# State-space chunk sums as three products of split factors, formed at the head of the next step

## What is computed

```python
dlast = jnp.exp(cum[:, :, -1:, :] - cum)
states = jnp.einsum('bcjh,bcjhn,bcjhp->bchpn', dtc * dlast, Bc, xc)
cdec = jnp.exp(cum[:, :, -1, :])
def step(s, inp):
    st, dc = inp
    return (dc[:, :, None, None] * s + st, s)
y_inter = jnp.einsum('bcihn,bchpn->bcihp', Cc * jnp.exp(cum)[..., None], prev)
y = (y_intra + y_inter).reshape(b, l, H, P) + Dp[None, None, :, None] * x
```

## Time and profile before

| | us |
|---|---|
| runs | 2136.83, 2136.99, 2141.14 (median 2136.99) |
| the profiled execution, whole | 2136.12 |
| its span, first to last instruction | 2134.4 |
| TensorE busy | 2080.5 (97%) |
| TensorE weight load | 1548.7 (73%) |
| VectorE busy | 1468.0 (69%) |
| ScalarE busy | 1331.0 (62%) |
| GpSimd busy | 866.3 (41%) |

### The profile page before, as it was taken

The page is one execution under the profiler, slowest core; times in us unless marked ns, Lnnn a source line. Parts: engine busy times, 40 slices in busy tenths (PEclk is TensorE's granted clock), DMA queues, the critical chain, the costliest instruction groups (busy, mean ns, idle before and its releaser), DMA issues.

```text
span 2134.4 us, 33703 instructions
## 1 busy us (share of the span) xinstructions
PE 2080.5 (97%) x12040; PEld 1548.7 (73%) x12040; DVE 1468.0 (69%) x1814; ACT 1331.0 (62%) x2368; POOL 866.3 (41%) x759
## 2 busy tenths in 40 slices
PE   6999999998999999999999999999999999999999
PEld 4644444487777777777777777777777777888887
DVE  4466666284668778778878778687787776555555
ACT  2255555543588887878878787887878783333222
POOL 1001111131147576666757657566676672000000
PEclk9999999999999999999999999999999999999999
DMA  3522222142545555555445455455455457545452
GB/s 132 184 76 68 82 74 62 40 153 89 124 130 163 155 165 160 159 155 178 146 151 177 147 168 161 146 166 168 147 166 169 150 189 258 153 148 148 143 183 89
DMA packets 182781, 305.34 MB, mean 143 GB/s; under 512 B 20416, under 2 KB 96704, under 8 KB 182496
## 3 DMA queue, kind: packets, MB, share of 16 engines
q1 hardware_dynamic: 182624, 303.29, 45.7%
HBM read 249.90 MB, written 53.06 MB: 142 GB/s over the span
## 4 chain that ended last, share of the span: by engine, by line
PE 70%; ACT 2%; DVE 1%; POOL 1%; issue 1%; DMA 0%; DVEq 0%; SPq 0%; POOLq 0%; ACTq 0%
PE ssm_pp L156 16%; PE ssm_pp L158 15%; PE ssm_pp L157 15%; PE ssm_py L1412 5%; PE ssm_py L1407 4%; PE ssm_pstate L1391 4%; PE ssm_turn L1368 2%; PE ssm_py L156 1%; PE ssm_py L158 1%; PE ssm_py L157 1%; PE ssm_pp L1351 1%; PE ssm_pstate L156 1%; PE ssm_pstate L158 1%; PE ssm_pstate L157 1%; PE ssm_turn L156 1%; PE ssm_turn L158 1%
## 5 line engine op out<-in xcount | busy, mean ns | idle before, releaser
L156 PE MATMUL ssm_pp<-xhi,ssm_lo 128*128 128x512 f32 x1192 | 479.4, 402 | 4.2 <-DVE ssm_bc L1636 3.5
L158 PE MATMUL ssm_pp<-xhi,ssm_hi 128*128 128x512 f32 x1192 | 466.0, 391 | 0.0
L157 PE MATMUL ssm_pp<-xlo,ssm_hi 128*128 128x512 f32 x1192 | 465.4, 390 | 0.0
L1524 ACT ACTIVATE ssm_sct<-ssm_cumb,ssm_gpar 128x128 f32<-128x128 f32 x1024 | 313.1, 390 | 69.9 <-DMA ssm_cumb<-dt_sums 48.0
L148 POOL TENSOR_TENSOR ssm_lo<-ssm_raw,ssm_hi 128x512 fp32r<-128x512 f32 x150 | 244.0, 1632 | 91.0 <-ACT ssm_hi L137 91.0
L156 PEld LDWEIGHTS ssm_pp<-xhi,ssm_lo 128*128 128x128 f32 x1192 | 224.0, 188 | 67.5 <-issue 18.7
L1636 DVE SCALAR_TENSOR_TENSOR ssm_xc<-ssm_pp,vectors,ssm_xc 128x1022 f32<-128x1022 f32 (+2 forms) x192 | 245.2, 1277 | 34.7 <-ACT ssm_xc L1478 30.0
L158 PEld LDWEIGHTS ssm_pp<-xhi,ssm_hi 128*128 128x128 f32 x1192 | 224.0, 188 | 48.1
L157 PEld LDWEIGHTS ssm_pp<-xlo,ssm_hi 128*128 128x128 f32 x1192 | 224.4, 188 | 42.7
L1671 DVE TENSOR_TENSOR ssm_sct<-ssm_sct,ssm_cbm 128x1024 f32<-128x1024 f32 x128 | 229.1, 1790 | 28.0 <-ACT ssm_sct L1531 28.0
L1813 POOL TENSOR_TENSOR ssm_go<-ssm_t,ssm_gt 128x512 f32<-128x512 f32 x128 | 165.0, 1289 | 171.1 <-DVE ssm_t L1707 171.1
(11 more groups left out here) (281 smaller groups left out, 4141.9 us busy)
## 6 DMA issues: line engine op xcount, KB each, us to landing
ssm_cumb<-dt_sums SPq DMA_DIRECT2D x96, 1024.0 KB, 5.9
ssm_raw<-w SPq DMA_DIRECT2D x150, 256.0 KB, 5.6
gated<-ssm_go SPq DMA_DIRECT2D x128, 256.0 KB, 4.3
ssm_cumb<-dt_sums SPq DMA_DIRECT2D x32, 512.0 KB, 4.0
ssm_gt<-w SPq DMA_DIRECT2D x64, 256.0 KB, 2.7
ssm_xc<-gated SPq DMA_DIRECT2D x32, 512.0 KB, 4.2
ssm_sct<-gated SPq DMA_DIRECT2D x32, 512.0 KB, 4.2
ffn_raw<-w SPq DMA_DIRECT2D x37, 256.0 KB, 2.7
```

The costliest lines, as they stand in the source:

```text
L156: pe.matmul(out, wlo, xhi, start=start, stop=False)
L157: pe.matmul(out, whi, xlo, start=False, stop=False)
L158: return pe.matmul(out, whi, xhi, start=False, stop=stop)
L1524: i = act.activation(sct[:, s % 2, h, :], cumb[:, s % 2, 0, h, :], ACT.Relu, scale=-1.0, bias=gpar[:, unit, 0, s % NTOK, h:h + 1])
```

## The change

- The state sum leaves scan. chunk_sum(g, s-1) forms it at the head of step s on TensorE, ahead of the first entry, as three float32r products of `bt_hi`, `bt_lo`, `xw_hi`, `xw_lo` (none crosses from one group to the next, since step 15 is a chunk 3).
- `xw` has one buffer instead of two. Its high part is a copy on ScalarE in step s behind a weight's high part and ahead of the lag activations; its low part is a subtraction on GpSimd in step s, behind the gate product of step s-1. Both have one buffer, which belonged to the weights of the time-step projection.
- The transposed B is copied as its high part by ScalarE; VectorE subtracts for its low part ahead of the mask, once a group, and `bt_done` moves to that.
- VectorE's state update of step s-1 moves behind scores of step s and the y sum of step s-1.
- Memory: small buffers of the last norm take other places, and the split of the LoRA product on ScalarE moves from step 14 to step 15 of the last group, with its operands where B's parts were.

```diff
@@ -1011,6 +1011,7 @@
         dt_act, dt_dve, dt_turned, dt_copied, cum_out, par_out = map(
             sem, "dt_act dt_dve dt_turned dt_copied cum_out par_out".split())
         pre_done = sem("pre_done")
+        bt_hi_done, xw_hi_done, xw_lo_done = map(sem, "bt_hi_done xw_hi_done xw_lo_done".split())
         rms_in, rms_sum, rms_std, rms_inv, rms_out = map(sem, "rms_in rms_sum rms_std rms_inv rms_out".split())
         cum_in = [sem(f"cum_in{i}") for i in range(2)]
         g_out = [sem(f"g_out{i}") for i in range(2)]
@@ -1022,7 +1023,8 @@
         gt = sb("gt", [P, 2, CU, T])
         bc = sb("bc", [P, 2, T])
         cc = sb("cc", [P, T])
-        btok = sb("btok", [P, NTOK, N])
+        sbr = lambda n, s: ctx.enter_context(nc.sbuf_tensor(f"ssm_{n}", s, F32R))
+        bt_hi, bt_lo = sbr("bt_hi", [P, NTOK, N]), sbr("bt_lo", [P, NTOK, N])
         cbm = sb("cbm", [P, NTOK, CS])
         gpar = sb("gpar", [P, 2, 3, NTOK, HU])
         cdec = sb("cdec", [P, 2, HU, NTOK])
@@ -1030,7 +1032,8 @@
         sct = sb("sct", [P, 2, HU, CS])
         cecl = sb("cecl", [P, 2, HU, CS])
         xp = sb("xp", [P, 2, CU * P])
-        xw = sb("xw", [P, 2, CU * P])
+        xw = sb("xw", [P, CU * P])
+        xw_hi, xw_lo = dt_feed.hi[:, 0, :], dt_feed.lo[:, 0, :]
         state = sb("state", [P, 2, CU * P])
         t2 = sb("t2", [P, 2, CU, CS])
         go = sb("go", [P, 2, CU, CS])
@@ -1039,9 +1042,10 @@
         na = sb("na", [P, 1])
         lc = sb("lora_coef", [P, 1])
         at_lora = LORA % feed.slots
-        h_hi = (feed.hi[:, at_lora, :], dt_feed.hi[:, 0, :])
-        h_lo = (feed.lo[:, at_lora, :], dt_feed.lo[:, 0, :])
-        rms = sb("rms", [P, 2, (G - 1) * T // P])
+        first_tokens = lambda x: x[:, 0:NC, :].rearrange("p c n -> p (c n)")
+        h_hi = (feed.hi[:, at_lora, :], first_tokens(bt_hi))
+        h_lo = (feed.lo[:, at_lora, :], first_tokens(bt_lo))
+        rms = c.causal[:, 0:2 * ((G - 1) * T // P)].rearrange("p (u n) -> p u n", u=2)
         rms_eps = sb("rms_eps", [P, 1])
         z, e_, dt, da = (xc[:, 1, i, :] for i in range(CU))
         cum = gt[:, 1, 3, :].rearrange("p (n t) -> p n t", n=NTOK)
@@ -1198,6 +1202,7 @@
         o.unit0_summed = lambda eng: eng.wait_ge(t2_done, G * NS - NTOK)
         o.unit1_gated = lambda eng: eng.wait_ge(g_done, G * NS)
         o.unit1_summed = lambda eng, early=0: eng.wait_ge(t2_done, G * NS - early)
+        o.eps = rms_eps
         o.scores_read = lambda eng: eng.wait_ge(y_done, G * NS)
         o.weights_split = lambda eng: eng.wait_ge(feed.lo_done, G * GT + NPRE + 1)
         o.base_copied = lambda eng: eng.wait_ge(pre_done, KT)
@@ -1293,6 +1298,7 @@
                         parameters(g + 1, 0)
                     if last and s == 8:
                         sp.wait_ge(var_out, 2 * (G - 1) * B * 16)
+                        sp.wait_ge(cb_done, G)
                         for unit in range(2):
                             sp.dma_start(rms[:, unit, :], over_partitions(c.var_dram[unit, 0:G - 1])
                                          ).then_inc(rms_in, 16)
@@ -1376,21 +1382,26 @@
                                    start=True, stop=True)
                 mm.then_inc(var_sum, 1)
 
-            def scan(g, s):
+            def chunk_sum(g, s):
+
                 t, ch = s % NTOK, s % NC
-                unit = 1 if s < NTOK else 0
-
                 summed = s >= NTOK or before(g, 0, 1) is not None
                 if ch < NC - 1:
-                    pe.wait_ge(xw_done, g * NCA + (carried(s) + 1))
+                    pe.wait_ge(xw_lo_done, g * NCA + (carried(s) + 1))
                     after(pe, state_done, g * NCA + carried(s))
                     if s == 0:
                         pe.wait_ge(bt_done, g + 1)
                     if s % NTOK == NC and summed:
                         after(pe, var_done, var_before(g, s))
-                    pe.matmul(p_state[:], btok[:, t, :], xw[:, s % 2, :], start=True, stop=True
-                              ).then_inc(states_done, 1)
-                elif summed and s % NTOK < NC:
+                    product(pe, p_state[:], bt_hi[:, t, :], bt_lo[:, t, :], xw_hi, xw_lo, True, True
+                            ).then_inc(states_done, 1)
+
+            def scan(g, s):
+                ch = s % NC
+                unit = 1 if s < NTOK else 0
+
+                summed = s >= NTOK or before(g, 0, 1) is not None
+                if ch == NC - 1 and summed and s % NTOK < NC:
                     pe.wait_ge(state_done, g * NCA + carried(s))
                     pe.wait_ge(sqs_done, g * NS + (0 if s < NTOK else NTOK))
                     squares(unit)
@@ -1440,6 +1451,8 @@
 
             def body(g, last):
                 for s in range(NS):
+                    if s > 0:
+                        chunk_sum(g, s - 1)
                     for e in at(s, last)[:1]:
                         entry(g, e, range(1) if last and e >= NE else range(B))
                     for e in at(s - 1, last):
@@ -1506,12 +1519,18 @@
                 act.wait_ge(bt_turned, g + 1)
                 after(act, states_done, g * NCA)
                 e = ENTRIES.index("turn B")
-                act.activation(btok[:].rearrange("p c n -> p (c n)"), slot(e), ACT.Copy).then_inc(bt_done, 1)
+                act.activation(bt_hi[:].rearrange("p c n -> p (c n)"), slot(e), ACT.Copy).then_inc(bt_hi_done, 1)
 
             def copy_c(g):
                 act.wait_ge(x_done, g * NCV + 2)
                 after(act, cecl_done, g * NCA)
                 act.activation(cc[:], bc[:, 1, :], ACT.Copy).then_inc(c_copied, 1)
+
+            def weighed_high(g, s):
+                if s % NC < NC - 1:
+                    act.wait_ge(xw_done, g * NCA + (carried(s) + 1))
+                    after(act, states_done, g * NCA + carried(s))
+                    act.activation(xw_hi, xw[:], ACT.Copy).then_inc(xw_hi_done, 1)
 
             def lags(g, s):
 
@@ -1544,6 +1563,7 @@
 
                 act.wait_ge(dt_dve, 6 + NTOK)
                 act.wait_ge(tile_done, G * GT + LORA + 1)
+                act.wait_ge(states_done, G * NCA)
                 for b in range(B):
                     act.activation(h_hi[b], pp[:, (NE + LORA) % 2, b, :], ACT.Copy, scale=lc[:, 0:1]
                                    ).then_inc(marks.lora_hi, 1)
@@ -1583,9 +1603,7 @@
                     for e in single(s - 1, last):
                         first_tap(g, e)
                     for e in at(s - 2, last):
-                        if last and e == NE + LORA:
-                            lora_high()
-                        elif last and e >= NE:
+                        if last and e >= NE and e != NE + LORA:
                             copy_pre(e - NE)
                     if s % NC == 0 and s % NTOK > 0 and (s > NTOK or before(g, 0, 1)):
                         copy_squares(g * 2 - 1 + s // NTOK, 1 - s // NTOK)
@@ -1597,6 +1615,9 @@
                     tiles = [r for r in (real(g, e, AHEAD) for e in at(s, last) if is_tile(e)) if exists(r, last)]
                     for r in tiles[:1]:
                         high(r)
+                    weighed_high(g, s)
+                    if last and s == NS - 1:
+                        lora_high()
                     if behind(g, s, 1, last):
                         lags(*behind(g, s, 1, last))
                     if before(g, s, 2):
@@ -1672,6 +1693,12 @@
                                   cbm[:, s % NTOK, :].unsqueeze(1).broadcast_to([P, HU, CS]), ALU.mult
                                   ).then_inc(st_done, 1)
 
+            def b_low(g):
+                dve.wait_ge(bt_hi_done, g + 1)
+                e = ENTRIES.index("turn B")
+                dve.tensor_tensor(bt_lo[:].rearrange("p c n -> p (c n)"), slot(e),
+                                  bt_hi[:].rearrange("p c n -> p (c n)").bitcast(F32), ALU.subtract).then_inc(bt_done, 1)
+
             def scaled(g, s):
 
                 n = g * NS + s
@@ -1741,17 +1768,17 @@
                             mv = dve.tensor_copy(par[:, :, i // 2, i % 2 * NC + q, :],
                                                  dt_bank(i)[:, q, :].rearrange("p (u h) -> p u h", h=HU))
                         mv.then_inc(dt_copied, 1)
+            b_low(0)
             mask(0)
             scaled(0, 0)
 
             def body(g, last):
                 for s in range(NS):
-                    if before(g, s, 1):
-                        advance(*before(g, s, 1))
                     grown(g, s)
                     scores(g, s)
                     if before(g, s, 1):
                         finish(*before(g, s, 1))
+                        advance(*before(g, s, 1))
                     if last and s == 10:
                         dve.wait_ge(rms_in, 32)
                         dve.memset(rms_eps[:], RMS_EPS)
@@ -1764,6 +1791,7 @@
                     for e in single(s - 1, last):
                         conv(g, e)
                     if s == NS - 1 and not last:
+                        b_low(g + 1)
```

(12 more changed lines are left out.)

## The result

The changed kernel took 2144.61 us (median of 11 runs, 2140.15 to 2147.02), the kernel before 2136.83 (11 runs beside them): a ratio of 1.0035, 95% interval 1.0027 to 1.0043. It is slower by 7.8 us. The profiled execution has a span of 2142.9 us against 2134.4.

What follows compares the result with a forecast made beforehand. TensorE, busy all 150.50 us of a full group, was taken as the bound. Seven groups' -1.1 and the last group's +0.5 gave -0.6 us on the profiled run's 2136.12, 0.9 below the median 2136.99: forecast 2136.4, range 2125 to 2149.

Steps and rivals of the forecast that it cites:

- TensorE's arithmetic: State sum on TensorE: f32 product 0.86 us out, three products 0.69 in; 0.165 a sum, 1.98 a group, 15.8 in all.
- rival (d): On TensorE each of three products pays 0.10 us extra for change of form, 0.07 a sum left; about 2145 us; chance 0.06.
- The walk through a middle group: Step-by-step waits at TensorE's heads: stalls give back 1.8 of 1.98 us, net -0.16 a group, -1.1 for seven groups.
- at nothing, until ScalarE is late: ScalarE's 96 new copies of 0.62 us, 7.4 us a group on 28.8 idle, were costed at nothing.
- the f32 product's removal is worth 0.86 us a step: On TensorE, steps with a state sum take 1.39 us from turning to y, those without 0.53; removal saves 0.86 us.
- The last group: Half-tile steps from the seventh: six subtractions add 7.6 us to GpSimd's busy queue; +2.5 us at the last y product.
- The tail: Behind the last y product, TensorE's own waits of 1.83 and 1.77 us swallow most of +2.5, leaving +0.5 us.
- The advance moved: VectorE's state update, 0.6 us of work, moves 3 to 4 us later; hidden, about 0.8 us early in step 2.
- Rival (c): GpSimd's queue becomes the bound, with waits at heads 9, 10, 11 too and groups above 151.5 us; 2151 us; chance 0.18.

Runs made afterwards that it cites:

- the run with these waits taken away: Changed kernel with its last group undone; other groups: subtraction before decay and gate product in steps 0, 1, 13, lags before the copy in step 14; 2136.37 us.
- The short additions of squares: Changed kernel with GpSimd's two additions of squares over 8 columns of 128 in the last group, sums wrong there; 2143.11 us.
- the one meant to decide it: Kernel of 2128.28 us with move and full split in the last group, the high part made there by VectorE instead of ScalarE's copy; 2145.60 us.
- the last group of +4.33 us: Changed kernel; in the last group the subtraction is on VectorE and the state update goes between grown and scores; 2141.26 us.
- the run of 2128.28 us: Kernel of 2136.37 us with, in middle groups' step 12, ScalarE's square and silus ahead of copying the sums of squares; last group still undone; ratio 0.9961.

## Why the prediction was wrong

I forecast 2136.4 us, with 0.26 for slower by over 0.2%; it is 2144.61, within the range, but 7.8 us slower where I had forecast no change that can be told from noise. Two waits that the walk did not foresee, in TensorE's and in ScalarE's timeline of after:

```profile
1334.44 0.50 PE L156 MATMUL ssm_pp<-xhi,ssm_lo 128*128 128x512 f32 x1 [0.47 <-ACT ssm_gt L1516]
```

```profile
1327.61 0.63 ACT L1533 ACTIVATE dtw_hi<-ssm_xw 128x512 fp32r<-128x512 f32 x1 [3.91 <-POOL ssm_xw L1818]
```

By the steps of the prediction:

- **TensorE's arithmetic: right.** Four steps without stalls, from one chunk 0 to the next, got 0.5 us shorter (three sums of 0.165), in every middle group. Starts are 0.23 apart, so rival (d) is out.
- **The walk through a middle group: near in its sum, wrong in its parts.** -0.16 forecast, +0.13 measured, 2.0 us of the miss over seven groups. Head 1 waits 0.32 (forecast 0.35), head 14 0.67 (0.85), head 2 some 0.1 by the length of the step (0.6). These waits and the next come to 1.6 of the 2.1 us by which a middle group misses TensorE's gain of 1.98; the rest is in steps that are longer without a wait that the profile names. Not forecast: the first tile of step 15 waits 0.47 us for its slot, on the silu of a gate tile, which stands in ScalarE's queue behind a copy that waited 3.91 us for GpSimd. That was the item costed "at nothing, until ScalarE is late". The waits are also not what holds the gain back by itself: the run with these waits taken away gained 0.2 us a group, because VectorE's convolution at step 14 was next. The step that failed here is the sentence that the f32 product's removal is worth 0.86 us a step wherever it stands: at step 14 the product covered a wait.
- **The last group: the term that was mis-sized.** +2.5 us forecast at the last y product, +7.8 measured (+8.7 in the window that holds one product more). I counted GpSimd's gaps ("0.4 too much if every gap is used, 4 if half of them are"). The short additions of squares show that its time has a small part at most, and leaving out single steps shows what has the large one: the copy, for which I had put down nothing, 3.75 us (some 2.0 without the low clock), and the subtraction 5.28. The two hang on chains through three queues, whose length I never compared with a step of half a tile. And I had no term for the clock: 1.6 of the 7.8 us are a stretch of TensorE at 0.50 behind the wait of 2.77 us.
- **The tail: wrong.** I let it swallow 2 of 2.5 us. After, the last y product is 7.9 us later than before by the time axis of the profile, and the first gated tile starts at 1787.72 instead of 1780.86, 6.9 later: it swallowed 1.0. Behind that tile another 1.6 us are lost, in the stretch at low clock shown above. The tail's waits (1.43 and 1.17, before 1.83 and 1.77) shrank by 1.0 us in all: the sum of squares that the first of them hangs on comes from the last y product itself.
- **The advance moved: hidden in middle groups as forecast, 2.81 us of y waits in the last group.** Putting it back costs more (+15.4, +12.2 without the low clock).
- Rival (c) named the right direction, by the wrong cause: middle groups above 151.5 us and waits at heads 9, 10 and 11 are not there.

**What stays open** is which closed chain sets the pace of the last group. Removals and undoing show the prices; they don't show the path. The traces are in keeping with a loop over two steps (weigh, copy, lags, square, exponential, scores, finish, gate product, squares, weigh), but this is argued and not shown: four runs that opened a side of it gained 0.7 us at most, even with the low clock taken off, and the one meant to decide it made a loop of its own. Why the clock falls behind some waits and not behind others stays open too. A full version with two buffers for the high part wasn't tried. Nor was a full version that combines the faster middle groups with the last group of +4.33 us. From the rows that would be 2128.3 + 3.4 = about 2132 us, an estimate: in the run of 2128.28 us the seventh and eighth groups take 150.09 + 116.88 us by their y products, and with that last group they would take 149.2 + 121.15.
